# Twenty tiles of an edge gather fetched row by row from SyncE's queue, through two side buffers

## What is computed

```python
h = (x @ W).reshape(n, H, C)                       # H = 4 heads, C = 64
al_src = jnp.einsum('nhc,hc->nh', h, a_src)
al_dst = jnp.einsum('nhc,hc->nh', h, a_dst)
e = jax.nn.leaky_relu(al_src[src] + al_dst[dst], 0.2)
emax = jax.ops.segment_max(e, dst, num_segments=n)
ee = jnp.exp(e - emax[dst])
denom = jax.ops.segment_sum(ee, dst, num_segments=n)
alpha = ee / (denom[dst] + 1e-16)
out = jax.ops.segment_sum(h[src] * alpha[:, :, None], dst, num_segments=n)
```

## Time and profile before

| what | value |
| --- | --- |
| time of three runs, median | 6411.74 us (6405.93 to 6443.31) |
| span of the profiled execution, first to last instruction | 5133.3 us |
| attention stage in it, first fetch to last score | 2400.8 to 4564.6 us |
| instructions | 76751 |
| busy: PE, DVE, ACT, POOL | 3775.5, 3388.9, 2416.2, 3451.8 us |
| issues of the fetch L1430 | 1712, mean 951 ns |

### The profile page before, as it was taken

The page is one execution under the profiler, slowest core; times in us unless marked ns, Lnnn a source line. Parts: engine busy times, 40 slices in busy tenths (PEclk is TensorE's granted clock), DMA queues, the critical chain, the costliest instruction groups (busy, mean ns, idle before and its releaser), DMA issues. The chain is left out here.

```text
span 5133.3 us, 76751 instructions
## 1 busy us (share of the span) xinstructions
PE 3775.5 (74%) x19865; PEld 2844.9 (55%) x19865; DVE 3388.9 (66%) x9213; ACT 2416.2 (47%) x7596; POOL 3451.8 (67%) x3620
## 2 busy tenths in 40 slices
PE   6277777777777777775676777777777777768998
PEld 4156666666566666654454555555555555545665
DVE  6655555555555555554788888888788888874454
ACT  5323333333333333333576666666666666661222
POOL 4377777777777777774777777777777777732222
PEclk9589999999999999898777677777677677768999
DMA  4655655656555566663555555555555555534221
GB/s 132 202 161 170 171 170 170 170 170 170 169 170 167 169 171 170 170 170 97 139 150 154 150 150 152 149 150 148 152 146 155 149 149 153 150 92 149 75 78 48
DMA packets 338812, 767.24 MB, mean 149 GB/s; under 512 B 79990, under 2 KB 178392, under 8 KB 338238
## 3 DMA queue, kind: packets, MB, share of 16 engines
q0 software_dynamic: 202704, 594.02, 41.8%
q1 hardware_dynamic: 135662, 168.07, 10.0%
HBM read 712.95 MB, written 58.60 MB: 150 GB/s over the span
## 5 line engine op out<-in xcount | busy, mean ns | idle before, releaser
L826 POOL DMA_INDIRECT flow_rows<-table,edges x1708 | 1625.4, 952 | 609.0 <-issue 499.0
L1430 POOL DMA_INDIRECT gat_steps_rows<-table,edges x1712 | 1627.7, 951 | 558.5 <-issue 488.1
L1864 PE MATMUL gat_steps_sum_ps<-gat_steps_rows,gat_steps_onehot 128*128 128x264 f32 x3424 | 1149.9, 492 | 270.4 <-DVE acc L1584 258.1
L1173 PE MATMUL flow_sum_ps<-flow_rows,flow_onehot 128*128 128x256 bf16 x5124 | 767.1, 290 | 430.3 <-DMA flow_rows<-table,edges 343.9
L1864 PEld LDWEIGHTS gat_steps_sum_ps<-gat_steps_rows,gat_steps_onehot 128*128 128x128 f32 x3424 | 780.9, 240 | 488.1 <-DVE acc L1584 302.1
L1173 PEld LDWEIGHTS flow_sum_ps<-flow_rows,flow_onehot 128*128 128x128 bf16 x5124 | 497.7, 104 | 628.4 <-issue 299.9
L1731 ACT ACTIVATE gat_steps_rows<-gat_steps_rows 128x64 f32<-128x64 f32 x3424 | 828.6, 334 | 0.0
L899 DVE TENSOR_TENSOR acc<-flow_sum_ps,acc 128x256 f32 x854 | 360.2, 422 | 659.8 <-PE flow_sum_ps L1173 638.7
L1584 DVE TENSOR_TENSOR acc<-gat_steps_sum_ps,acc 128x264 f32 x856 | 370.1, 432 | 275.6 <-PE gat_steps_sum_ps L1864 200.6
L1225 PE MATMUL flow_y_ps<-flow_w,flow_hid 128*128 128x256 f32 x1568 | 434.9, 402 | 85.8 <-DVE flow_x_blk L985 44.7
L1215 PE MATMUL flow_hid_ps<-flow_xn_t,flow_w 128*128 128x128 f32 x3136 | 457.2, 293 | 11.1 <-ACT flow_hid L1108 10.9
(11 more groups left out here) (382 smaller groups left out, 5390.7 us busy)
## 6 DMA issues: line engine op xcount, KB each, us to landing
gat_steps_drow<-drow SPq DMA_DIRECT2D x107, 512.0 KB
gat_steps_rows<-table,edges POOLq DMA_INDIRECT x1712
flow_rows<-table,edges POOLq DMA_INDIRECT x1708, 3.1
expert_w<-in_L_ffn_w SPq DMA_DIRECT2D x16, 1024.0 KB, 7.4
table<-start_parts SPq DMA_DIRECT2D x49, 192.0 KB, 1.8
gat_steps_mask<-masks SPq DMA_DIRECT2D x428, 12.1 KB
table<-flow_row SPq DMA_DIRECT2D x49, 130.0 KB, 2.5
gat_steps_self_row<-table SPq DMA_DIRECT2D x49, 130.0 KB
```

What stands on the lines that cost most here:

```text
L826: nc.gpsimd.indirect_dma_start(out=rows[n % RING][:, t, :], out_offset=None, in_=g["table0"][:, :], in_offset=bass.IndirectOffsetOnAxis(ap ...
L1173: ins = t.matmul(sum_ps[i % 2][:, :], onehot[i // AHEAD % 2][:, i % AHEAD * T + u, :], rows[i % RING][:, u, part * D:(part + 1) * D], star ...
L1430: nc.gpsimd.indirect_dma_start(out=rows[w % RING][:, t, 0:RW], out_offset=None, in_=g["table1"][:, :], in_offset=bass.IndirectOffsetOnAxis ...
L1864: ins = t.matmul(sum_ps[(w * SPW + s) % BANKS][:, :], onehot[k][:, i, :], rows[r][:, i, :], start=(i == s * T), stop=(i == s * T + T - 1))
```

## The change

At three places of each of the seven groups of 128 steps (steps 42, 84 and 126 of the group, as far as they exist: 20 steps in all) the second tile of the step is no longer fetched by GpSimd. SyncE fetches it instead: it loads the 128 row numbers into registers, eight at a time, and issues one DMA of one row (1040 bytes) for each, into one of two side buffers `single[k]`. When the ring's place is free, one more DMA copies the side buffer into the ring (`place`), and ACT's `scores` waits for that copy (`placed`) in place of the fetch. The numbers come from `single_src`, a small table that `start_phase` writes to device memory after the edges have come in. `lines(j, part)` issues 32 rows (PART) after the `load` of each of four successive waves, from the sixth to the third before the wave of the tile; for the first tile, in wave 5, parts 0 and 1 are both issued in turn 0 of SyncE's loop, between `load(0)` and `load(1)`.

```diff
--- before.py
+++ after.py
@@ -44,6 +44,7 @@
 E = 8
 NEG = -1.0e38
 F = 1024
+SINGLE_AT, SINGLES = (42, 84, 126), [q * P + p for q in range(SQ) for p in (42, 84, 126) if q * P + p < STEPS - 1]
 CAP = -(-5 * NODES // (4 * E))
 PITCH = -(-CAP // P) * P
 
@@ -278,6 +279,7 @@
         edges_kept = sem("edges_kept")
         masks_ready = sem("masks_ready")
         masks_out = sem("masks_out")
+        singles_out = sem("singles_out")
         span_in = sem("span_in")
         flags_ready = sem("flags_ready")
         w_turned = sem("w_turned")
@@ -334,6 +336,10 @@
             for m in range(SETS):
                 for i, at in enumerate(rows_of(nc, sp, g, m * SET, SET, 0)):
                     sp.dma_start(g["x"][:, m * SET + i, :], a["x"][bass.ds(at, P), :]).then_inc(x_in[m], 16)
+            sp.wait_ge(edges_in, 32 * SQ)
+            pitch = SINGLE_AT[1] - SINGLE_AT[0]
+            assert all(p == SINGLE_AT[0] + i * pitch for i, p in enumerate(SINGLE_AT))
+            sp.dma_start(g["single_src"][:, :, :], src_s[SINGLE_AT[0]:SINGLE_AT[-1] + 1:pitch, :, P:2 * P]).then_inc(singles_out, 16)
             with nc.allow_non_contiguous_dma(reason="the ends of each tile"):
                 for n in range(2):
                     sp.dma_start(g["ends"][n:n + 1, 0:1], zero_row[:, 0:1]).then_inc(masks_out, 16)
@@ -360,6 +366,7 @@
             for k in range(DEEP):
                 sp.wait_ge(rows_out[k], 16 * len(range(k, NB, DEEP)))
             sp.wait_ge(masks_out, 16 * 7)
+            sp.wait_ge(singles_out, 16)
 
         @block.vector
         def _(dve):
@@ -1297,6 +1304,8 @@
         drow = [sb(f"drow{k}", [P, W * P], BF16) for k in range(2)]
         mask = [sb(f"mask{k}", [WH, MASK], BF16) for k in range(2)]
         flags = [sb(f"flags{k}", [1, 4, H, W]) for k in range(2)]
+        single = [sb(f"single{k}", [P, RW]) for k in range(2)]
+        single_at = [sb(f"single_at{k}", [1, P], I32) for k in range(2)]
         score = [sb(f"score{k}", [P, H, W]) for k in range(2)]
         pre_max = sb("pre_max", [WH, P])
         run_max = sb("run_max", [WH, P])
@@ -1359,6 +1368,9 @@
         own = sem("own")
         rows_in = [sem(f"rows_in{k}") for k in range(RING)]
         flags_in = [sem(f"flags_in{k}") for k in range(2)]
+        single_at_in = [sem(f"single_at_in{k}") for k in range(2)]
+        single_in = [sem(f"single_in{k}") for k in range(4)]
+        placed = sem("placed")
         onehot_t_ready = sem("onehot_t_ready")
         onehot_ready = sem("onehot_ready")
         scores_ready = sem("scores_ready")
@@ -1420,6 +1432,10 @@
 
         assert all(begins(k + 1) - begins(k) >= 6 for k in range(NB - 1))
         LAST_TICK = begins(NB - 1) + STAGES
+        by_sync = [s * T + T - 1 for s in SINGLES]
+        AHEAD, BATCH = 7, 8
+        PART = -(-P // (BATCH * (AHEAD - 2))) * BATCH
+        assert all(b // W - a // W >= AHEAD - 2 for a, b in zip(by_sync, by_sync[1:])) and by_sync[0] >= (AHEAD - 2) * W
 
         @block.gpsimd
         def _(pool):
@@ -1427,6 +1443,8 @@
                 w, t = divmod(n, W)
                 if w >= RING and t % T == 0:
                     pool.wait_ge(summed, n // T - RING * SPW + 1)
+                if n in by_sync:
+                    continue
                 nc.gpsimd.indirect_dma_start(
                     out=rows[w % RING][:, t, 0:RW], out_offset=None, in_=g["table1"][:, :],
                     in_offset=bass.IndirectOffsetOnAxis(ap=index[:, n:n + 1], axis=0)).then_inc(rows_in[w % RING], 16)
@@ -1455,16 +1473,59 @@
                 sp.dma_start(g["ends_x"][bass.ds(at, P), 0:D], x_new[:, :]).then_inc(stored, 16)
                 sp.dma_start(g["ends_x"][bass.ds(at, P), D:2 * D], tile_at(g["acc"], k, RA)[:, 0:D]).then_inc(stored, 16)
 
+            def number(j):
+                q, p = divmod(by_sync[j] // T, P)
+                if j >= 2:
+                    sp.wait_ge(single_in[(j - 2) % 4], 16 * P * ((j - 2) // 4 + 1))
+                sp.dma_start(single_at[j % 2][:, :], g["single_src"][SINGLE_AT.index(p), q:q + 1, :]).then_inc(single_at_in[j % 2], 16)
+
+            def lines(j, part):
+                if part == 0:
+                    sp.wait_ge(single_at_in[j % 2], 16 * (j // 2 + 1))
+                    if j >= 2:
+                        sp.wait_ge(placed, 16 * (j - 1))
+                for at in range(part * PART, min((part + 1) * PART, P), BATCH):
+                    _, numbers = nc.values_load_multi_w_load_instructions(
+                        single_at[j % 2][0:1, at:at + BATCH], engines=[sp.engine], min_val=0, max_val=NB * P - 1,
+                        skip_runtime_bounds_check_because="a node's number")
+                    for p, number_ in enumerate(numbers, at):
+                        sp.dma_start(single[j % 2][p:p + 1, :], g["table1"][bass.ds(number_, 1), :]).then_inc(single_in[j % 4], 16)
+
+            def place(j):
+                w, t = divmod(by_sync[j], W)
+                sp.wait_ge(single_in[j % 4], 16 * P * (j // 4 + 1))
+                at_least(sp, summed, (w - RING) * SPW + (t // T) + 1)
+                sp.dma_start(rows[w % RING][:, t, 0:RW], single[j % 2][:, :]).then_inc(placed, 16)
+
+            def singles(w):
+                for j, n in enumerate(by_sync):
+                    if n // W == w + 1:
+                        place(j)
+                        if j + 2 < len(by_sync):
+                            number(j + 2)
+                for j, n in enumerate(by_sync):
+                    part = w - (n // W + 1 - AHEAD)
+                    if w == 0 and part > 0:
+                        for early in range(part):
+                            lines(j, early)
+                    if 0 <= part < AHEAD - 2:
+                        lines(j, part)
+
             with nc.allow_non_contiguous_dma(reason="the gate's 8 columns"):
                 for t, src in ((gamma[:, :], a["L1_gnn_gamma"].partition_broadcast(P)),
                                (gate[:, :, :], a["L1_ffn_gate_w"].rearrange("(c p) e -> p c e", p=P)),
                                (gate_b[:, :], a["L1_ffn_gate_b"].partition_broadcast(P))):
                     sp.dma_start(t, src).then_inc(gates_in, 16)
+            number(0)
+            number(1)
             fetch(0)
             load(0, 0)
+            singles(0)
             load(1, 1)
+            singles(1)
             for w in range(2, NW):
                 load(w, w % 2)
+                singles(w)
                 for k in range(NB):
                     if begins(k) + 6 == (w - 2) * TICKS + begins(k) % TICKS:
                         store(k)
@@ -1703,7 +1764,10 @@
 
             def scores(w, k, r, trips):
 
-                act.wait_ge(rows_in[r], trips * (16 * W))
+                theirs = sum(n // W <= w and n // W % RING == r for n in by_sync)
+                act.wait_ge(rows_in[r], 16 * (trips * W - theirs))
+                if any(n // W == w for n in by_sync):
+                    act.wait_ge(placed, 16 * sum(n // W <= w for n in by_sync))
                 at_least(act, arg_ready, w - 1)
                 s.copy(score[k][:, :, :].rearrange("p h t -> p t h"), scores_of(r)).then_inc(scores_ready, 1)
 
@@ -2282,6 +2346,7 @@
              "masks": nc.dram_tensor("masks", [SQ * P * T, MASK], BF16).ap(),
              "drow": nc.dram_tensor("drow", [SQ * P, GROUP], BF16).ap(),
              "ends": nc.dram_tensor("ends", [2, 1 + SQ * P * T], F32).ap(),
+             "single_src": nc.dram_tensor("single_src", [len(SINGLE_AT), SQ, P], I32).ap(),
              "flags": nc.dram_tensor("flags", [NW, 4 * H * W], F32).ap(),
              "ends_x": nc.dram_tensor("ends_x", [NB * P, 2 * D], F32).ap(),
              "iota": sb("iota", [P, P]), "pidx": sb("pidx", [P, 1]),
```

## The result

The changed kernel takes 6528.69 us (median of 4 runs, 6507.73 to 6538.89), the kernel before 6415.59 (four runs, 6405.93 to 6443.31): ratio 1.017, interval 1.0149 to 1.0191. That is 54 us above the upper end of the range.

A forecast was written before the change was run, and what follows sets the result against it. It took the attention stage's arithmetic order (VectorE, PE, ACT; 20.2 us a slot) as the bound, GpSimd's fetches within 1%. Terms -1 + 2 + 4 = +5 us on the timed 6411.74 gave 6417, range 6378 to 6475.

The forecast's parts named there:

- 1278.4 us of that lie in no row: Sum: timed median 6411.74 against span 5133.3; this difference kept unchanged when adding +5 us to reach 6417.
- Code outside the span: Rival: about 8000 added instructions lengthen the 1278 us around the span by 10.4%, +133 us, 6550; chance 0.04.
- Does it fit: SyncE in the attention stage: own work plus rows need 93 to 98 of 107.8 us a tile, 86 to 91%.
- The sign of being wrong: Mid attention stage: VectorE waiting for `drow` or ACT for `self_row`, or slots below 20.0 us, would refute the forecast.
- SyncE becomes the bound: Rival: a row costs SyncE over 0.66 us; +20 to +130, both causes 300, priced +75, 6487; chance 0.16.
- its two causes: SyncE rival: a register load of eight costs about 1.5 us, or a row issues like a mask DMA.
- my value: SyncE's register load of eight row numbers, put at 0.58 us with its gap.
- my 70 to 75.5: SyncE's us for one tile: 16 loads of 0.58 plus 128 rows of 0.474 to 0.517.
- Two slips in the working: GpSimd's late fetches put at one every 1.268 us; SyncE's tile with mask-like issues summed as 109.6 us.
- -1 and +6 for the two halves: Removing 20 GpSimd fetches gains 1 us; SyncE's added work costs 2 for late fetches and 4 at the start.
- The late start: Attention stage start: 64 rows before `load(1)` make wave 1's scan 8 to 10.5 us late; end 0 to 11 late, taken +4.
- GpSimd is the bound in the timed runs: Rival: arithmetic is quicker without the profiler, so all 20 x 1.25 = 25 us come off, 6387; chance 0.13.

The follow-up runs named there:

- run 16: The kernel before, unchanged, run again for a trace at the slower pace: 6399.48 us, span 6397.6.
- 12: The kernel before, unchanged, run again for its trace: 5135.79 us.
- 14: Changed kernel with its 2560 row DMAs at fixed addresses, without register loads and address operations: 5125.82 us, ratio 0.9986 to the kernel before.
- run 5: The whole change again, beside the kernel before: 5132.65 us, ratio 0.9993 (0.9983 to 1.0003).
- run 15: Changed kernel plus two register loads, each with a row DMA using its value, per eight rows: 5612.04 us, ratio 1.0941 to the kernel before.
- run 17: Changed kernel with fixed-address row DMAs, no register loads or operations, where the kernel before takes 6393.85 us: 6285.71 us, ratio 0.9833.
- 8: The whole change once more, where the kernel before takes 6399.88 us: 6585.78 us, ratio 1.0277.
- 18: Changed kernel plus one register load with one row DMA per eight rows, same chip as run 17: 6839.94 us, ratio 1.0708 to the kernel before.
- run 4: Changed kernel with one DMA of 128 fixed neighbouring rows per tile: 5131.91 us, ratio 0.9998 to the kernel before; one execution took 6284.07.

## Why the prediction was wrong

**The step that failed** is in the sum: "1278.4 us of that lie in no row, and I leave them as they are". I took them for time around the span, and priced a rival on that (*Code outside the span*, which has no ground: run less span is 1.8 us). They were rows all the time: executions at another pace, longer in every stage but the last (run 16: 6399.48 us, span 6397.6). From it followed the second failure, in "Does it fit": 86 to 91% of SyncE's queue was worked out from a quick execution, where SyncE isn't free for 431 us of the stage; on a slow chip it is 1552, before any row is added. A trace that is 20% shorter than the time it is to explain is of another condition; the forecast should have asked which of its terms scale with it. The sign of being wrong that the forecast named, VectorE waiting for `drow`, is there (72.6 us in 12 waits between 3100 and 5900 us); ACT waits for `x_mid`, which the same `fetch` brings, instead of `self_row`.

**The criterion fits, its numbers didn't.** The rival *SyncE becomes the bound* says: decide by what a row may cost, (interval of a tile less SyncE's own work) / 128. Taking the stage less SyncE's waits as the time that SyncE isn't free:

| | stage | SyncE not waiting | for a row | limit for a row |
|---|---|---|---|---|
| quick, before (12) | 2140 | 431 | | 0.67 |
| quick, fixed rows (14) | 2134 | 1216 | 0.31 | |
| quick, change (5) | 2137 | 1807 | 0.54 | |
| quick, two more loads and rows (15) | 2622 | 2520 | 0.82 | |
| slow, before (16) | 2891 | 1552 | | 0.52 |
| slow, fixed rows (17) | 2783 | 2165 | 0.24 | |
| slow, change (recorded; 8) | 3027; 3085 | 2921; 2993 | 0.53; 0.56 | |
| slow, one more (18) | 3330 | 3260 | 0.67 | |

A row's figure is the difference to the kernel before over 2560; the limit is the stage of before less its SyncE time over 2560. The kernels that lost, and only these, are over the limit; but that is no second proof, since by this subtraction a kernel is over it whenever its stage grew by more than the waits it has left. What is measured is that of these kernels each that lost has only 70 to 106 us of SyncE's waits left, and each other one 330 or more. What moved it is not the rows (0.54 quick, 0.53 to 0.56 slow) but SyncE's own work: 431 us on the quick chip, 1552 on the slow one for the same 1383 instructions. Slots a third longer gave SyncE 751 us more, and its own stretched queue took 1121. I had allowed for neither. (Late semaphores and the steps of 0.7 us that the view of waits doesn't list count as SyncE's time here, so the figures are what it can't use, not what it works.)

The rival's price, +75 out of +20 to +130, stood for an overrun at the quick pace; its two causes (a dear register load, a dear issue) aren't what happened, so that +113 lies in its range is luck. The register load was dearer than my value, 0.782 us against 0.58, but far from the rival's 1.5, the row was cheaper, 0.412 against 0.474 to 0.517, and a tile came to 16 x 0.81 + 128 x 0.412, some 66 us, under my 70 to 75.5. The Trainium skill, "Runtime: NRT & Kernel Launch", section "Instruction fetch mechanics", with its 200 ns a register, would put this load at an estimated 1.6 us; the traces have half of that, 0.782. Two slips in the working change nothing: the fetches of the last 73 slots come every 1.255 us and not 1.268, as that stretch holds 14.6 us behind the last fetch, and 9.3 + 77 + 22.8 is 109.1, not 109.6.

**What held, on quick chips.** -1 and +6 for the two halves: measured 0.9985 and 1.0013, -6 and +6 us by the medians. The whole: +5 forecast, -5.5 measured, with an interval (-9 to +2) that doesn't reach the +5: "within 1%" held, the sign didn't. The late start: the scan of wave 1 was forecast 8 to 10.5 us late; it is 6 (2450.33, 48.6 us into the stage against 42.6), and it is caught up by wave 5 (its score copy begins 121.9 us into the stage, 121.8 before), so my +4 was 0. On slow chips the 64 rows take 100.64 us instead of some 33 (60 of them took 31.06 in run 5), and the 6 are 29 us.

**GpSimd.** The rival *GpSimd is the bound in the timed runs* (6387) has its sign in run 17: without the register work the change gains 108 us on a slow chip. That is luck, for GpSimd isn't the bound there: it waits 580 us for the sums (33 on the quick chip), and 20 x 1.25 = 25 us of its queue don't make 108. (The lone 6284.07 of run 4 is near run 17's time, but its granted clock, 0.645, is not: 0.761 to 0.771.) The saving shows as less waiting for late semaphores, ACT from 774 to 545 us and VectorE from 597 to 488. Why fewer fetches, or a busier SyncE, should make semaphores less late is open; only whole kernels were compared, and no run removed tiles without adding rows there.

So the loss on the slow chips is shown to be SyncE's queue without room, filled by the register work of the rows on top of the rows: it goes when the register work goes (17), grows when loads and rows are added (18), and the same waits appear on a quick chip once its queue is filled (15). The division of the recorded 113 us is by subtraction: about 110 gained by what gains in run 17, about 220 lost on SyncE, 29 of these at the start. The lengths of the slots from one score copy to the next speak for it: in run 17 the median is 26.2 us and one in ten takes 29.5 or more, so the change's ordinary slot has run 17's gain, and its loss lies in some long slots. What makes an execution slow, and SyncE's instructions come in steps of 0.7 us, was not tried. Every timed execution here carries a span, so whether the steps are the chip's or the recording's can't be told either.

## What to carry to other kernels

Put the span of the trace beside the median of the timed runs first; if they differ by more than a few us, the trace is of another condition, and every "it fits" must be worked out again with the waits, not the durations, of a trace at the right time. A queue that is 85% full on the quick chip (1807 of 2137 us) is full on the slow one, where even instructions of 29 ns are stretched. So an idle queue is better given few instructions than a register load and an address for each row: with fixed addresses the rows fitted at both paces (14, 17); one DMA for each tile was run on quick chips only. And before an added load that has no effect is believed, count its instructions in the trace.

## Unexpected behaviour of the hardware

- Two paces, 5130 and 6400 us for one program, with busy times of VectorE, ACT and GpSimd in the attention stage that are equal within 0.5%; the granted clock there is 0.72 and 0.67, in the convolution 0.92 and 0.82, and 0.98 for both in the last stage, which takes 482 us at either.
- On slow chips an engine waits up to 12.7 us for a semaphore that comes late (ACT in run 16, 96 waits, 774 us in all), and moves and register operations of 29 and 37 ns take up to 1.4 us, in steps of 0.7 (466 of SyncE's 1383 instructions in the attention stage of run 16 end one or two such steps after the one before, 11 in the quick trace of the same kernel); GpSimd's fetches keep their length, 954 ns against 951.
- A one-row DMA with a register address takes SyncE 0.412 us from row to row (37 + 29 + 228 ns and gaps), a register load of eight 0.782. In run 15 loads of which only the first number is used take 0.527 in the median, those of which only the second is used 0.749.
